# Rotary queries computed transposed in an f32 attention block: transposes out of TensorE, rotary sum to VectorE

## The reference, cut to what matters

```
c_q    = x @ w_q_down                      # 192 wide
q_nope = c_q @ w_q_up_nope; q_rope = rope(c_q @ w_q_up_rope)   # per head 128 and 64
c_kv   = x @ w_kv_down;     k_rope = rope(x @ w_k_rope)        # 64 and 64, all heads
q_lat  = q_nope @ w_uk[h]                                      # 64
scores = (q_lat @ c_kv.T + q_rope @ k_rope.T) / sqrt(192), causal
out    = softmax(scores) @ c_kv @ w_uv[h].T, then all heads @ w_out
rope(x1, x2) = x1*cos - x2*sin, x1*sin + x2*cos                # halves of 32
```

## Time and profile before

| what | us |
|---|---|
| median of 3 runs | 1309.1 (1309.09 to 1309.19) |
| profiled execution | 1308.3 |
| its span, first to last instruction | 1306.3 |
| TensorE busy | 1196.5 (92%) |
| TensorE weight loads | 1007.7 (77%), beside the matmuls |
| VectorE busy | 849.7 (65%) |
| ScalarE busy | 639.9 (49%) |
| GpSimd busy | 510.1 (39%) |
| mean granted TensorE clock | 0.978 of full speed |

### The profile page before, as it was taken

One profiled execution on the slowest core, in us unless ns is written; L12 is line 12 of the kernel. 1 busy time (PEld: TensorE's weight loads), 2 busy tenths in 40 slices (PEclk: granted clock), 3 DMA queues, 4 the chain that ended last, 5 costly groups with the idle time before them and its releaser, 6 DMA issues.

```text
span 1306.3 us, 27806 instructions
## 1 busy us (share of the span) xinstructions
PE 1196.5 (92%) x8424; PEld 1007.7 (77%) x8424; DVE 849.7 (65%) x3281; ACT 639.9 (49%) x1818; POOL 510.1 (39%) x798
## 2 busy tenths in 40 slices
PE   5988999999896999999988799999979789999996
PEld 4657788887695788888777688888869678888876
DVE  4756666665774666666666566666667566666755
ACT  3645555555133555555413455555522465555541
POOL 1405444444212544454312354544521254444531
PEclk9999999999898999999989899999999999999998
DMA  8630000000100000000100000000010000000000
GB/s 260 203 117 2 1 1 0 0 2 2 33 33 3 2 1 1 0 1 2 34 31 3 3 2 1 1 0 2 2 33 33 1 1 2 1 0 0 3 1 33
DMA packets 21487, 27.64 MB, mean 21 GB/s; under 512 B 10198, under 2 KB 11990, under 8 KB 20730
## 3 DMA queue, kind: packets, MB, share of 16 engines
q1 hardware_dynamic: 19002, 21.45, 5.3%
q10 hardware_dynamic: 2368, 4.72, 1.1%
HBM read 21.97 MB, written 4.19 MB: 20 GB/s over the span
## 4 chain that ended last, share of the span: by engine, by line
PE 72%; issue 13%; DVE 9%; ACT 2%; POOL 2%; SPq 1%; DMA 1%; POOLq 0%; DVEq 0%; ACTq 0%
PE Y L893 13%; PE Y L867 10%; PE XZ L852 9%; PE Y L801 9%; PE XZ L831 5%; PE XZ L833 5%; PE XZ L832 5%; PE Y L581 4%; PE XZ L581 3%; PE Y L813 3%; PE XZ L560 1%; DVE qT_lo L1444 1%; DVE stats L1144 1%; DVE small L1496 1%; DVE XZ L1496 1%
## 5 line engine op out<-in xcount | busy, mean ns | idle before, releaser
L541 POOL TENSOR_TENSOR prob<-prob,small 128x512 f32<-128x512 f32 (+3 forms) x512 | 360.6, 720 | 440.1 <-DVE small L1451 439.4
L1496 DVE CUSTOM_DVE_ANT_0 XZ<-XZ,mask 128x512 f32<-128x512 f32 (+3 forms) x512 | 244.3, 508 | 289.1 <-issue 285.6
L1116 ACT ACTIVATE prob<-XZ,small 128x512 f32<-128x512 f32 (+3 forms) x512 | 266.6, 525 | 290.9 <-DVE small L1496 290.9
L831 PE MATMUL XZ<-kT_hi,qT_hi 128*128 128x512 f32 (+3 forms) x512 | 186.2, 364 | 25.0 <-DVE qT_lo L1444 14.9
L852 PE MATMUL XZ<-ident,prob 128*128 128x128 f32 x1280 | 195.5, 275 | 0.2
L833 PE MATMUL XZ<-kT_hi,qT_lo 128*128 128x512 f32 (+3 forms) x512 | 166.9, 326 | 0.0
L832 PE MATMUL XZ<-kT_lo,qT_hi 128*128 128x512 f32 (+3 forms) x512 | 166.1, 324 | 0.0
L852 PEld LDWEIGHTS XZ<-ident,prob 128*128 128x128 f32 x1280 | 147.6, 140 | 21.1 <-POOL prob L541 7.4
L867 PE MATMUL Y<-probT,ckv 128*64 128x384 f32 (+2 forms) x1280 | 152.3, 384 | 8.6 <-ACT probT L366 8.0
L366 ACT ACTIVATE probT<-XZ 128x512 f32<-128x512 f32 x192 | 114.6, 597 | 86.1 <-PE XZ L852 83.8
L485 POOL TENSOR_TENSOR q_tok<-q_tok,q_sin 128x256 f32<-128x256 f32 x128 | 93.4, 730 | 131.3 <-DVE q_sin L1436 130.8
(11 more groups left out here) (200 smaller groups left out, 2500.9 us busy)
## 6 DMA issues: line engine op xcount, KB each, us to landing
wout_nat<-in_L_attn_w_out_dram SPq DMA_DIRECT2D x16, 512.0 KB, 4.3
out_dram<-x_sb SPq DMA_DIRECT2D x16, 256.0 KB, 2.0
x_next<-_attn_hidden_states_dram SPq DMA_DIRECT2D x12, 256.0 KB, 3.1
wbase_nat<-in_L_ffn_W_base_dram ACTq DMA_DIRECT2D x1, 1024.0 KB, 5.5
x_sb<-_attn_hidden_states_dram ACTq DMA_DIRECT2D x4, 256.0 KB, 7.1
nope_a<-_L_attn_w_q_up_nope_dram ACTq DMA_DIRECT2D x1, 1024.0 KB, 6.2
rope_a<-_L_attn_w_q_up_rope_dram SPq DMA_DIRECT2D x1, 1024.0 KB, 10.2
rope_bb<-_L_attn_w_q_up_rope_dram SPq DMA_DIRECT2D x2, 512.0 KB, 12.9
```

Of the source, the lines that this page charges most:

```text
L541: last = nc.gpsimd.tensor_tensor(prob[u % RING][:, c:c + w], prob[u % RING][:, c:c + w], inv_sum[:, u % RING, m:m + 1].broadcast_to([P, w] ...
L831: nc.tensor.matmul(bank[:, c:c + w], high, kT_hi[:, 0:w], start=True, stop=False)
L1116: last = nc.scalar.activation(prob[u % RING][:, c:c + w], score_ps[u % 2][:, c:c + w], ACT.Exp, bias=neg_max[:, u % RING, m:m + 1], scale= ...
L1496: last = nc.vector.tensor_tensor_reduce(bank, bank, mask[:, S - w:S], -1.0, HIGHEST, ALU.add, ALU.min, neg_max[:, u % RING, m:m + 1])
```

## The change

Queries are made transposed. `q_products` holds the weights of one head stationary and streams 512 tokens, so the 128 parts of a head's query lie on partitions: 0 to 63 the latent part, 64 to 95 and 96 to 127 the two rotary halves. One bank per head. VectorE multiplies all 128 partitions by a table (ones for the latent part, cosines below), the two rotary quarters crosswise by the sines, waits for that, and adds on 64 partitions. ScalarE takes the high part from this sum in SBUF, GpSimd the low part. The query transposes, the latent copy and GpSimd's addition are gone. `q_turned` and `q_sums` lie where `qT_hi` and `qT_lo` lie. ScalarE copies all five probability banks. For pair 0 of a batch each head is made in two parts, 384 tokens before the last key tile is transposed and 128 behind it. The four bodies of `attention` are written out without the inner loop. Three small tables are loaded and one memset is added in the opening. Bodies of functions that are replaced stand above and are left out here:

```diff
+cosT = np.cos(angle).astype(f).T
+sinT = np.sin(angle).astype(f).T
+return (np.ascontiguousarray(cos), np.ascontiguousarray(np.stack([sin, -sin], axis=2)),
+    np.ascontiguousarray(cosT), np.ascontiguousarray(np.concatenate([sinT, -sinT], axis=0)))
...
-q_tok = place("q_tok", [P, 2, 2, HD], F32, rb)
-q_sin = place("q_sin", [P, 4, 2, HALF], F32, rb)
+cosT = place("cosT", [P, S], F32, after_outputs)
+sinT = place("sinT", [P, S], F32, after_outputs)
+after_scores, turned_home = [after_outputs[0]], [after_outputs[0]]
+qT_hi = [place(f"qT_hi{i}", [P, 2, S], F32R, after_outputs) for i in range(2)]
+qT_lo = [place(f"qT_lo{i}", [P, 2, S], F32R, after_outputs) for i in range(2)]
+q_turned = [place(f"q_turned{i}", [P, 2, S], F32, turned_home) for i in range(2)]
+q_sums = [place(f"q_sums{i}", [P, 2, S], F32, turned_home) for i in range(2)]
...
-def attention(b, slot_work, tail):
-    for u in range(BODY):
-        slot_work(0, u)
-    with loop(b[1], 1, BODIES - 1) as g:
-        for u in range(BODY):
+def attention(slot_work, tail):
+    for g in range(BODIES):
+        for u in range(BODY + (tail if g == BODIES - 1 else 0)):
             slot_work(g, u)
-    for u in range(BODY + tail):
-        slot_work(BODIES - 1, u)
...
+EARLY, LATE = slice(0, 3 * P), slice(3 * P, S)
+FIRST_PARTS = ((0, EARLY), (1, EARLY), (0, LATE), (1, LATE))
+def q_index(b, n, head):
+    return 34 * b + 2 + 2 * n + head
...
+            sp.dma_start(sinT[64:P, :], rope_sinT).then_inc(turns_in, 16)
+            for j in range(2):
+                sp.dma_start(cosT[64 + 32 * j:96 + 32 * j, :], rope_cosT).then_inc(turns_in, 16)
...
-        def halves(b, n, half):
...
+        def qT_low(m, head, par, cols=slice(0, S)):
+            pool.wait_ge(qT_hi_set, m + 1)
+            nc.gpsimd.tensor_tensor(qT_lo[par][:, head, cols], q_sums[par][:, head, cols],
+                                    f32(qT_hi[par][:, head, cols]), ALU.subtract).then_inc(qT_lo_set, 1)
+        def first_queries(b):
+            m = q_index(b + 1, 0, 0) - 2
+            for j, (head, cols) in enumerate(FIRST_PARTS):
+                qT_low(m + j, head, 0, cols)
...
-                if u % UNITS in (0, 2) and within(g, u, UNITS * LAST_PAIR - 1):
-                    halves(b, BODY_PAIRS * g + u // UNITS + 1, (u % UNITS) // 2)
+                k, p = u % UNITS, u // UNITS
+                if k in (1, 3) and within(g, u, UNITS * LAST_PAIR - 1):
+                    qT_low(q_index(b, BODY_PAIRS * g + p + 1, k // 2), k // 2, (p + 1) % 2)
...
         def first_queries(b):
             pe.wait_ge(x_updated, 8 * b + 4 + DOWN)
-            q_products(b + 1, 0, 0, True)
-            transpose_down(b, STEPS - 1)
-            q_transposes(b + 1, 0, 0, True)
-            pe.wait_ge(ckT_hi, 4 * (b + 2))
-            pe.wait_ge(ckT_lo, 4 * (b + 2))
-            q_products(b + 1, 0, 1, False)
-            q_transposes(b + 1, 0, 1, False)
+            pe.wait_ge(ckT_hi, 4 * (b + 2) - 1)
+            pe.wait_ge(ckT_lo, 4 * (b + 2) - 1)
+            m = q_index(b + 1, 0, 0) - 2
+            for j, (head, cols) in enumerate(FIRST_PARTS):
+                if j == 2:
+                    transpose_down(b, STEPS - 1)
+                    pe.wait_ge(ckT_hi, 4 * (b + 2))
+                    pe.wait_ge(ckT_lo, 4 * (b + 2))
+                q_products(m + j, 0, head, cols, bank_free=(j >= 2 or not first(b + 1)))
...
-        def q_products(b, n, half, opening):
...
+        def q_products(m, n, head, cols=slice(0, S), bank_free=True):
+            if bank_free:
+                pe.wait_ge(q_rot_set, m - 1)
+            hi, lo, rest = (w[:, 2 * n + head, :]
+                            for w in (wq1_hi, wq1_lo, wq2))
+            parts = ((hi, cq_hi[:, 0, cols]), (lo, cq_hi[:, 0, cols]), (hi, cq_lo[:, 0, cols]),
+                     (rest, cq_hi[:, 1, cols]), (rest, cq_lo[:, 1, cols]))
+            for j, (w, c) in enumerate(parts):
+                last = nc.tensor.matmul(qT_ps[head][:, cols], w, c, start=(j == 0), stop=(j == 4))
             last.then_inc(q_done, 1)
-        def q_transposes(b, n, half, opening):
...
         def scores(b, g, u):
             n = 80 * b + BODY * g + u
-            pair = 16 * b + BODY_PAIRS * g + u // UNITS
-            if u % UNITS == 0:
-                pe.wait_ge(qT_hi_set, 2 * pair + 2)
-                pe.wait_ge(qT_lo_set, 2 * pair + 2)
+            if u % UNITS < 2:
+                pe.wait_ge(qT_lo_set, q_index(b, BODY_PAIRS * g + u // UNITS, u % UNITS) + 1)
...
         def transpose_probs(b, g, v):
             pe.wait_ge(prob_scaled, 80 * b + BODY * g + v + 1)
             if known(g, v, 2):
-                by_act, by_dve = bank_copies(b, g, v - 2)
-                if (v - 2) % UNITS in ACT_BANKS:
-                    pe.wait_ge(probT_by_act, by_act)
-                else:
-                    pe.wait_ge(probT_by_dve, by_dve)
+                pe.wait_ge(probT_set, 80 * b + BODY * g + v - 1)
             for h, i, c in MEMBERS[v % UNITS]:
                 for j in range(i + 1):
                     at = slice(c + j * P, c + (j + 1) * P)
...
         def pv(b, g, p):
             pair = 16 * b + BODY_PAIRS * g + p
-            by_act, by_dve = bank_copies(b, g, UNITS * p + UNITS - 1)
-            pe.wait_ge(probT_by_act, by_act)
-            pe.wait_ge(probT_by_dve, by_dve)
+            pe.wait_ge(probT_set, UNITS * (pair + 1))
...
-                    q_products(b, n, k // 2, False)
+                    q_products(q_index(b, n, k // 2), n, k // 2)
                 if k == PV_SLOT and known(g, u, UNITS):
                     pv(b, g, p - 1)
                 if known(g, u, T_LAG) and within(g, u, SLOTS - 1 + T_LAG):
                     transpose_probs(b, g, u - T_LAG)
                 if output_rows(u) is not None and known(g, u, 3 * UNITS):
                     output(b, g, p, output_rows(u))
-                if k in (1, 3) and queries:
-                    q_transposes(b, n, k // 2, False)
...
-        def q_latent(b, n, half):
...
-        def qT_high(b, n, half, par):
...
+        def qT_high(m, head, par, cols=slice(0, S)):
+            act.wait_ge(q_sum_set, m + 1)
+            nc.scalar.activation(qT_hi[par][:, head, cols], q_sums[par][:, head, cols],
+                                 ACT.Copy).then_inc(qT_hi_set, 1)
+        def copy_probT(b, g, v):
+            act.wait_ge(probT_done, 80 * b + BODY * g + v + 1)
+            if known(g, v, UNITS):
+                act.wait_ge(pv_done, 16 * b + BODY_PAIRS * g + v // UNITS)
+            nc.scalar.activation(probT_unit(v), bank_unit(v), ACT.Copy).then_inc(probT_set, 1)
...
-                    qT_high(b, n1, k // 2 - 1, (p + 1) % 2)
-                if k in (1, 3) and queries:
-                    q_latent(b, n1, k // 2)
+                    qT_high(q_index(b, n1, k // 2 - 1), k // 2 - 1, (p + 1) % 2)
...
-                if known(g, u, T_LAG) and within(g, u, SLOTS - 1 + T_LAG) and v % UNITS in ACT_BANKS:
-                    copy_probT(act, nc.scalar, b, g, v)
-            attention((b, act), work, TAIL)
+                if known(g, u, T_LAG) and within(g, u, SLOTS - 1 + T_LAG):
...
         def first_queries(b):
-            q_rotary(b + 1, 0, 0)
-            ckT_low(b, STEPS - 1)
-            qT_low(b + 1, 0, 0, 0)
-            q_rotary(b + 1, 0, 1)
-            qT_low(b + 1, 0, 1, 0)
+            m = q_index(b + 1, 0, 0) - 2
+            for j, (head, cols) in enumerate(FIRST_PARTS):
+                if j == 2:
+                    ckT_low(b, STEPS - 1)
+                q_rotary(m + j, head, 0, cols)
...
-        def q_rotary(b, n, half):
...
+        def q_rotary(m, head, par, cols=slice(0, S)):
             dve.wait_ge(q_done, m + 1)
-            if not (isinstance(n, int) and n == 0 and half == 0):
-                dve.wait_ge(qT_done, m)
-            for tt in range(2):
-                t = 2 * half + tt
-                q = q_ps[:, tt * 256:(tt + 1) * 256].rearrange("p (h r) -> p h r", h=2)[:, :, KVL:HD] \
-                    .rearrange("p h (k f) -> p h k f", k=2)
-                nc.vector.tensor_tensor(q_tok[:, tt, :, KVL:HD].rearrange("p h (k f) -> p h k f", k=2), q,
-                                        cos_sb[:, t, :].unsqueeze(1).unsqueeze(1).broadcast_to([P, 2, 2, HALF]),
-                                        ALU.mult)
-                last = nc.vector.tensor_tensor(q_sin[:, 2 * tt:2 * tt + 2, :, :], q,
-                                               sin_sb[:, t, :, :].unsqueeze(1).broadcast_to([P, 2, 2, HALF]),
-                                               ALU.mult)
-            last.then_inc(q_rot_set, 1)
-        def qT_low(b, n, half, par):
...
+            bank = qT_ps[head]
+            q, turned = q_sums[par][:, head, cols], q_turned[par][:, head, cols]
+            nc.vector.tensor_tensor(q, bank[:, cols], cosT[:, cols], ALU.mult)
+            nc.vector.tensor_tensor(turned[64:96, :], bank[96:P, cols], sinT[96:P, cols], ALU.mult)
```

(51 more changed lines are left out.)

71 lines of the change are left out of this document (18 added, 53 removed).

## The result

The change makes the kernel slower by 0.5%: 1316.1 us median (1313.7 to 1318.0, five runs) against 1309.2, ratio 1.005 with a 95% interval of 1.0035 to 1.0065. Forecast was no change, 1309. The number is near; the terms are not. Two large ones were missed, and they nearly cancel: that the sum came near is luck.

The account below looks back on a forecast made before the run. Two nearly level paths bound it: TensorE's own work, and scores, reduction, exponential, copy, PV. Sum 1308.3 - 3 - 4.5 + 4 + 3.5 = 1308.3, with the median's 0.8, 1309 us; range 1280 to 1336.

Parts of the forecast that it names:

- First pairs of a batch: First four pairs of each batch: 56.8 us against 55.8, +1.0 per batch, +4 us in all, bounds -4 and +8.
- Loops unrolled: Attention bodies written out without the inner loop: -4.5 us, or 0 if straight code stalls as well.
- Steady pairs: Pairs 4 to 14 of each batch: 14.68 us against 14.75, 44 x -0.07 = -3 us.
- other pairs: Row for all pairs behind the first five, four batches: 636.0 us before, 628.7 forecast.
- Between batches: Opening and ways between batches: two rotations queue on VectorE ahead of the last key's low part, +3.5 us, bounds 0 and +8.
- The hidden terms: Work changes on ScalarE, VectorE and GpSimd: none has as much work as TensorE, their order is what matters.
- the walk: Steady pair followed instruction by instruction: rotation 2.27 to 5.11, reduction 1 at 5.11, PV at 9.16, pair 14.68 us.
- The rivals: Three alternatives to the walked case: TensorE regains its work (0.25), VectorE waits for GpSimd (0.18), straight code stalls (0.05).
- get its work back: Rival in steady pairs: quarter-partition instructions overlap, 1293 us, or the stream bound holds, 1280 us; chance 0.25.
- Straight code: Rival at the 16 body starts: each stalls 0.3 to 0.5 us, 1317 to 1321 us; chance 0.05.
- GpSimd's contention: Rival at VectorE's rotation addition: it waits up to 1.19 us for GpSimd, 1360 us, half of it 1334; chance 0.18.

Follow-up runs that it names:

- e3_fill: Kernel after with 27 matmuls per batch added, product unread, where TensorE waits for ScalarE in the first three pairs: 1303.7 us, ratio 0.9953.
- e4_split: Kernel after with head 0's high part moved behind slot 2's bank copy on ScalarE, and VectorE's reduction 1 put ahead of the rotation: 1275.9 us, ratio 0.9740.
- e1_before_straight: Kernel before with the four attention bodies written out, without the inner loop: 1297.2 us, ratio 0.9902 to the kernel before.
- e2_high_later: Kernel after with ScalarE's high part of head 0 moved behind slot 2's bank copy, GpSimd's low part one slot on: 1291.0 us, ratio 0.9853.
- e5_loops_of_three: Kernel after with the inner loop back on VectorE, ScalarE and GpSimd, TensorE kept straight: 1319.1 us, ratio 1.0069 to the kernel before.
- e7_key_first: Kernel after with the last key tile's low part moved on VectorE behind head 0's 384-token rotation: 1312.1 us, ratio 1.0021.

## Why the forecast missed

- **First pairs of a batch: wrong, the step that failed.** "It gives 13.7, 13.0 and 14.2 for the three and 15.9 for the fourth" is right for each pair in which the clock does not fall anew (pair 0 starts at the lower level in both kernels): batch two has 13.86, 13.17 and 15.70 for the first, second and fourth, batch three 14.23 for the third. But I priced TensorE's waits of 1.3 to 1.9 us as waits alone. They let the granted clock fall to 1.2 GHz, and PV takes 2.2 us more at that level, ahead of everything else in its pair; where the fall struck pair 1 it cost 1.3 to 1.5. The first five pairs cost 11.8 us more than forecast, 14.1 more than before, outside the bounds of -4 to +8 for that term. The e3_fill run shows the cause. In the kernel before, the 1.32 us wait of the earlier trace rows stands at the head of pairs 1 to 3, with no other above 0.7 us in the pair, and no PV ran at the lower level.
- **Loops unrolled: too small.** Forecast -4.5, read from twelve pairs of one batch; alone it is -11.6, also in the first pairs, in the last batch and between batches.
- **Steady pairs: the path right, the part behind PV not.** PV at 9.14 against 9.16. From PV to the next pair it takes 5.34 instead of 5.52. The query transposes are gone from there, 0.36, and so are 0.08 that the probability transposes need longer ahead of them (505.36 to 505.85 before, 511.44 to 511.85 now); the scores of slot 0 follow the last output matmul by 0.23 instead of 0.32, and why wasn't tested. The -0.20 on 40 pairs would be -8 us, and the row "other pairs" is off by 7.2: the edges in it gave 1.2 more than forecast, and against that the last batch, written out, was at 14.59 without the change.
- **Between batches: +6.0 against +3.5, within its bounds.** Sized against the kernel before. Against that kernel written out it is +8.2 (opening 0.9, between batches 7.0, tail 0.3): a longer queue on VectorE, partly hidden in the count because the old loop's 2.2 us went away.
- **The hidden terms.** That ScalarE's own share does not matter was right; that its order does was in the walk and not followed up. Both moves of e4_split can be read off the walked pair.
- **The rivals.** TensorE did not get its work back: PV waits 0.90. Straight code does not stall: no hole at a body start, all later pairs 14.48. GpSimd's contention exists, at the place named, and is covered as worked out (next but one section). None of the rivals was the fall of the clock.

The kernel after is thus what e1_before_straight gives, 1297.2, and 19 us on top of it. In spans it is 17.0: +17.5 in the first five pairs, +8.2 between batches and at the ends, -8.8 in the other pairs, where the change does what it was counted to do.

## What to carry to other kernels

Where a change makes TensorE wait in a place where it had little idle time, price the wait and then the work behind it at 1.2 GHz, and try cheap matmuls in the hole before judging the change. Measure a structural side effect, such as written-out loops, by itself: here it was worth more than the change it came with and hid what the rest cost. When a wait takes over, walk the engine in front of it for instructions that nobody is waiting for and move those behind: two moves were worth 40 us, about a third of it in the first pairs.

## What the runs showed of the hardware

- VectorE and GpSimd block each other at SBUF, both ways. The addition with two SBUF inputs takes 0.69 us with GpSimd idle and 1.26 with one in flight:

```profile
509.31 1.26 DVE L1403 TENSOR_TENSOR q_sums<-q_sums,q_turned 64x512 f32<-64x512 f32 x1
...
508.98 1.04 POOL L542 TENSOR_TENSOR prob<-prob,small 128x512 f32<-128x512 f32 x1
```

  and in e4_split, where the addition (492.92) is 0.05 us ahead, it keeps its 0.69 and GpSimd's scaling takes 1.54 instead of 1.04. That is the rule of the Trainium skill, "SBUF — State Buffer", Who interferes with whom: the one that comes later waits. Reduction 3 starts at 510.70, right behind the held addition, and PV (to 511.5) covers it. Of the 120 additions of this width in the kernel after 52 last over 1.1 us, in e4_split none.
- An instruction on 32 partitions costs what one on 128 does (0.69 and 0.68 us), and with the partitions changing from one to the next nothing overlaps: 0.70 us from start to start for 512 elements, which a row at 256 elements had told.
- The return of an outer loop can be dear because of an inner one: 3.22 and 3.16 us of "issue" against 1.50 on data.
- A fall of the clock moves. In the profiled executions of the kernel after and of e2_high_later, e3_fill, e5_loops_of_three and e7_key_first it struck a PV in two to six places each, in pairs 1 to 3, and in e5_loops_of_three also at a loop's edge and in pair 14 of the last batch; this fits the kernel after's spread of 4.3 us over its runs, though only one of those runs has a profile.
